# A graph layer's sixty-four-node blocks built in groups of three, with the gather sums in the same ring of PSUM banks

## The reference

```
x: (12500, 128) f32;  src, dst, edge_type: (400000,) int32;  W_data, W_control, W_self: (128, 128)
Xs     = x[src]
m_data = Xs @ W_data.T + b_data
m_ctrl = Xs @ W_control.T + b_control
msg    = where(edge_type == 0, m_data, m_ctrl)
agg    = segment_sum(msg, dst, num_segments=12500)
out    = relu(agg + x @ W_self.T + b_self)
result = layernorm(x + out)          # over the features, no scale or shift
```

## Time and profile before

| | us |
|---|---|
| median of 3 runs | 2782.12 |
| lowest and highest run | 2778.26, 2785.72 |
| the profiled execution, its time | 2784.88 |
| the profiled execution, its span | 2783.0 |
| TensorE busy in the span | 2364.6 |
| VectorE, ScalarE, GpSimd busy | 1266.1, 1224.5, 1691.7 |

### The profile page before, as it was taken

How to read it: one execution, slowest core, us unless ns; L and a number is a source line. 1 busy time by engine, 2 the same in 40 slices (tenths; PEclk the granted TensorE clock), 3 DMA queues, 4 the chain that set the end, 5 groups by cost and what they waited for, 6 DMA issues and landing times.

```text
span 2783.0 us, 47819 instructions
## 1 busy us (share of the span) xinstructions
PE 2364.6 (85%) x17776; PEld 1301.3 (47%) x17776; DVE 1266.1 (45%) x4037; ACT 1224.5 (44%) x1997; POOL 1691.7 (61%) x1785
## 2 busy tenths in 40 slices
PE   3688888888888888888889888988888888888988
PEld 2344444544444444444445454444444444444444
DVE  8444444445444444444444454444444444444443
ACT  6344444444444444444444444444444444444443
POOL 6466665666666665666666666566666666656662
PEclk9899999999999999999999999999999999999999
DMA  7712222222222222222222222222222222222221
GB/s 191 223 47 67 71 72 59 73 68 74 72 73 71 73 72 62 74 69 75 71 72 73 69 75 71 63 69 73 74 69 73 71 73 72 69 61 72 71 75 34
DMA packets 150380, 211.42 MB, mean 76 GB/s; under 512 B 35298, under 2 KB 120725, under 8 KB 150147
## 3 DMA queue, kind: packets, MB, share of 16 engines
q0 software_dynamic: 83232, 170.57, 22.0%
q1 hardware_dynamic: 54177, 28.15, 3.7%
q10 hardware_dynamic: 12738, 9.60, 1.1%
HBM read 189.78 MB, written 18.41 MB: 75 GB/s over the span
## 4 chain that ended last, share of the span: by engine, by line
PE 44%; another core or an unknown queue 23%; ACT 14%; DVE 9%; issue 7%; DVEq 2%; DMA 1%; SPq 0%; ACTq 0%
PE apply_ps L664 25%; ACT cnt L860 13%; PE build L648 8%; PE sum_ps L630 4%; DVEq L1177 2%; DVE hot_q L1136 2%; DVE hot_p L1136 1%; PE misc L673 1%; DVE acc L1183 1%; PE misc L714 1%; DVE sg L1193 1%; PE misc L717 1%; DMA key_dram<-fin 1%; PE misc L692 1%
## 5 line engine op out<-in xcount | busy, mean ns | idle before, releaser
L560 POOL DMA_INDIRECT rows<-x_dram,src_t x1610 | 1524.7, 947 | 947.5 <-issue 383.4
L860 ACT ACTIVATE cnt<-build 128x784 bf16<-128x784 f32 x1408 | 1087.5, 822 | 1457.1 <-remote 773.1
L664 PE MATMUL apply_ps<-x,cnt 128*128 128x385 bf16 x8624 | 1611.2, 337 | 31.0 <-issue 25.5
L664 PEld LDWEIGHTS apply_ps<-x,cnt 128*128 128x128 bf16 x8624 | 868.3, 103 | 604.7 <-issue 135.7
L648 PE MATMUL build<-hot_q,hot_p 64*128 64x196 bf16 x5632 | 425.1, 254 | 274.2 <-ACT cnt L860 205.6
L648 PEld LDWEIGHTS build<-hot_q,hot_p 64*128 64x128 bf16 x5632 | 197.6, 95 | 572.7 <-issue 372.7
L1136 DVE TENSOR_TENSOR hot_q<-const_ps,key_pq 128x784 bf16<-128x784 bf16 x704 | 390.3, 554 | 0.0
L1181 DVE TENSOR_TENSOR acc_deg<-misc,acc_deg 2x32 f32 x346 | 61.9, 179 | 671.2 <-remote 278.7
L1136 DVE TENSOR_TENSOR hot_p<-const_ps,key_pq 128x512 bf16<-128x512 bf16 x704 | 291.2, 414 | 43.1 <-DVE acc L1183 16.5
L560 POOL DMA_INDIRECT rows<-in_x,src_t x120 | 122.8, 1024 | 76.8 <-issue 30.5
L1191 DVE TENSOR_TENSOR zg<-t_mask,sum_ps 128x2 f16<-128x2 f32 x161 | 24.9, 154 | 307.5 <-PE sum_ps L630 158.3
(11 more groups left out here) (182 smaller groups left out, 1082.5 us busy)
## 6 DMA issues: line engine op xcount, KB each, us to landing
rows<-x_dram,src_t POOLq DMA_INDIRECT x1610
x_dram<-x ACTq DMA_DIRECT2D x13, 672.0 KB
cnt<-in_x SPq DMA_DIRECT2D x13, 448.0 KB
x_u<-in_x SPq DMA_DIRECT2D x43, 64.0 KB
out<-out_sb SPq DMA_DIRECT2D x43, 64.0 KB
key_dram<-fin SPq DMA_DIRECT2D x12, 196.5 KB
x_u<-in_x SPq DMA_DIRECT2D x40, 53.5 KB
out<-out_sb SPq DMA_DIRECT2D x40, 53.5 KB
```

The source lines that it names most:

```text
L560: pool.indirect_dma_start(out=rows_f[:, slot, 0:D] if early else rows[:, slot, 0:ROW], out_offset=None, in_=x if early else x3_dram, in_of ...
L664: last = pe.matmul(apply_ps[:, 0:385], cnt[:, k % 2, b, :], x3[:, b, 0:385], start=(b == 0), stop=(b == XBLOCKS - 1))
L860: act.activation(o, i.rearrange("p h (m b) -> p b h m", b=XBLOCKS), ACT.Copy).then_inc(evacuated, 1)
```

## The change

The PSUM tensor of the tables and that of the gather sums go. The tables of line 1136 lie in an SBUF tensor `tables`, and the one of line 1041 in `hot_t`. The four banks become six: `build_ps[0]` to `[2]`, two banks each, used in turn by a list of entries. An entry is a build (now one j) or the sums of a round, in the order in which TensorE makes them; each waits until the entry three before it has been copied out (`evacuated` for a build, `sg_ready` for sums).

Builds come in groups of three, that is twelve nodes. With step s = 3m the group 6m, 6m + 1, 6m + 2 is built at the old place, ahead of the job. With s = 3m + 1 the group 6m + 3 to 6m + 5 is built in the middle of `apply`, which is cut into two halves. With s = 3m + 2 there is none. ScalarE copies the first group out ahead of the step's job and the second behind it.

```
+    def group_at(s):
+        lo = {0: 2 * s, 1: 2 * s + 1}.get(s % 3, 2 * BATCHES)
+        return range(lo, min(lo + 3, 2 * BATCHES))
...
+    entries = []
+    for s in range(STEPS):
+        if s in gather_at:
+            entries.append(("sums", gather_at[s]))
+        entries += [("build", j) for j in group_at(s)]
+    entry = {v: e for e, v in enumerate(entries)}
...
+        hot_t = sb("hot_t", [P, 2 * WIN])
+        tables = sb("tables", [P, P + 2 * XBLOCKS, 2], BF16)
...
-        const_ps = psum("const_ps")
-        build_ps = [psum(f"build{i}", 2 * WIDE) for i in range(2)]
+        build_ps = [psum(f"build{i}", 2 * WIDE) for i in range(BUFFERS)]
         apply_ps = psum("apply_ps")
-        sum_ps = psum("sum_ps")
...
+            def free_banks(who):
+
+                e = entry[who]
+                if e >= BUFFERS:
+                    kind, n = entries[e - BUFFERS]
+                    pe.wait_ge(sg_ready if kind == "sums" else evacuated, n + 1)
+                return build_ps[e % BUFFERS]
...
                 pe.wait_ge(hot_ready, ps + 1)
-                if ps:
-                    pe.wait_ge(sg_ready, ps)
+                if ps == 0:
+                    pe.wait_ge(lists_stored, 2 * len(LISTS))
+                sum_ps = free_banks(("sums", ps))
...
-            def build(n):
-
-                pe.wait_ge(onehot_ready, n + 1)
-                for z in range(2):
-                    j = 2 * n + z
-                    if j >= 2:
-                        pe.wait_ge(evacuated, j - 1)
...
+            def build(j):
+
+                n, z = divmod(j, 2)
                 pe.wait_ge(onehot_ready, n + 1)
+                to = free_banks(("build", j))
+                for i in range(2):
+                    for h in range(2):
+                        half = slice(64 * h, 64 * h + 64)
+                        o = WIDE * h + 2 * XBLOCKS * i
+                        last = pe.matmul(to[:, o:o + 2 * XBLOCKS], hot_p[half, j % 8, :, i],
+                                         hot_q[half, j % 8, :, i], start=True, stop=True)
+                last.then_inc(built, 1)
...
-                b0, b1 = XBLOCKS * c // 8, XBLOCKS * (c + 1) // 8
+                b0, b1 = XBLOCKS * (2 * c + half) // 16, XBLOCKS * (2 * c + half + 1) // 16
...
-                if batch_at(s) is not None:
-                    build(batch_at(s))
+                if s % 3 == 0:
+                    for j in group_at(s):
+                        build(j)
...
-                if 0 <= k < BLOCKS:
-                    apply(k, c)
+                for half in range(2):
+                    if 0 <= k < BLOCKS:
+                        apply(k, c, half)
+                    if half == 0 and s % 3 == 1:
+                        for j in group_at(s):
+                            build(j)
...
-                if batch_at(s) is not None:
-                    evacuate(batch_at(s))
+                if s % 3 == 0:
+                    for j in group_at(s):
+                        evacuate(j)
...
                 if s in turn_at:
                     take_x(turn_at[s])
+                if s % 3 == 1:
+                    for j in group_at(s):
+                        evacuate(j)
...
-            dve.tensor_copy(const_ps[:, HOT], hot_i[:, :])
-            twice_p, twice_q = twice[:, 0:P, :], twice[:, P:P + 2 * XBLOCKS, :]
+            dve.tensor_copy(hot_t[:, :], hot_i[:, :])
             for r in range(2):
-                dve.tensor_copy(twice_p[:, :, r], iota_q[:, 0:P])
-                last = dve.tensor_single_scalar(twice_q[:, :, r], iota_q[:, :], 1.0, ALU.add)
-            step(last)
-            dve.tensor_copy(const_ps[:, TABLES], twice.rearrange("p w r -> p (w r)").bitcast(F32))
+                dve.tensor_copy(table_p[:, :, r], iota_q[:, 0:P])
+                dve.tensor_single_scalar(table_q[:, :, r], iota_q[:, :], 1.0, ALU.add)
```

More of the change, by code:

```diff
@@ L632, in gather_sums, with apply @@
                 last.then_inc(rows_used, 1)
-            def build(n):
+            def build(j):
+                n, z = divmod(j, 2)
                 pe.wait_ge(onehot_ready, n + 1)
-                for z in range(2):
-                    j = 2 * n + z
-                    if j >= 2:
-                        pe.wait_ge(evacuated, j - 1)
[L641 to L652, removed]
-                if c == 0:
+                to = free_banks(("build", j))
[6 more added lines that the diff above has]
+                last.then_inc(built, 1)
+            def apply(k, c, half):
+                if c == 0 and half == 0:
                     pe.wait_ge(evacuated, 16 * (k + 1))
@@ L665, in apply @@
                                      start=(b == 0), stop=(b == XBLOCKS - 1))
-                if c == 7:
+                if c == 7 and half == 1:
                     last.then_inc(applied, 1)
@@ L842, in take_sums @@
                 act.wait_ge(rows_used, ps + 1)
+                sum_ps = build_ps[entry["sums", ps] % BUFFERS]
                 act.activation(sg[:, ps % 2, :], sum_ps[:, 0:D + 1], ACT.Copy).then_inc(act_step, 1)
@@ L846, in take_sums, with evacuate @@
                                scale=sg[:, ps % 2, D:D + 1]).then_inc(sg_ready, 1)
-            def evacuate(n):
-                k = n // 8
-                if n % 8 == 0 and k >= 2:
+            def evacuate(j):
+                k = j // 16
+                if j % 16 == 0 and k >= 2:
                     act.wait_ge(applied, k - 1)
-                if n == 8:
+                if j == 16:
                     act.wait_ge(x3_ready, XCH)
-                for z in range(2):
-                    act.wait_ge(built, 2 * n + z + 1)
-                    c0 = 8 * (2 * (n % 8) + z)
-                    o = cnt[:, k % 2, :, c0:c0 + 8].rearrange("p b (h m) -> p b h m", h=2)
-                    i = build_ps[z][:, :].rearrange("p (h c) -> p h c", h=2)[:, :, 0:4 * XBLOCKS]
-                    act.activation(o, i.rearrange("p h (m b) -> p b h m", b=XBLOCKS), ACT.Copy
-                                   ).then_inc(evacuated, 1)
+                act.wait_ge(built, j + 1)
+                c0 = 8 * (j % 16)
+                o = cnt[:, k % 2, :, c0:c0 + 8].rearrange("p b (h m) -> p b h m", h=2)
+                i = build_ps[entry["build", j] % BUFFERS][:, :].rearrange("p (h c) -> p h c", h=2)[:, :, 0:4 * XBLOCKS]
+                act.activation(o, i.rearrange("p h (m b) -> p b h m", b=XBLOCKS), ACT.Copy).then_inc(evacuated, 1)
             def take_block(k):
```

15 lines of the change are left out of this document (7 added, 8 removed).

## The result

The kernel after takes 2899.95 us (median of 3 runs, 2887.93 to 2904.72) against 2782.12: ratio 1.042, 95% interval [1.036, 1.047], 4% slower where 2% faster was forecast, and outside the range. Its profiled execution took 2887.93 us with a span of 2886.1, at a mean granted clock of 0.94.

What follows compares the result with a forecast made beforehand. No engine is full; TensorE mostly waits for build banks that ScalarE copies late. Terms: -251 us bank waits, -40 insertions, +241 new waits, net -50, so 2782 becomes 2732, rounded 2730 us; range 2600 to 2850.

Steps and rivals of the forecast that it cites:

- Jobs behind three copies: Steps s = 3m, ScalarE copies three builds ahead of the job's bank: 49 waits for `misc`, 29 us more.
- Where s = 3m + 1 the job goes first, which is no worse: Steps s = 3m + 1, ScalarE copies the job out ahead of the group: no added cost.
- a wait also lets the others catch up: Sum of waits: reckoning gave 321 where rows have 251, so excesses of 200 were scaled by 0.78 to 156 us.
- The lag: From the end of a step's first four build matmuls to ScalarE's start: mean 1.23 us, taken as given.
- 62 x 0.78: Plain groups without sums next to them: 297 groups at 0.21 us mean excess, 62 us, scaled by 0.78.
- the third build at s = 0: Third build needs the sums' own banks and waits for VectorE's reduce: 58 x 1.47 = 85 us.
- the sums at s = 8: Sums need the bank of the group's first build, 0.6 us of room: 57 x 0.81 = 46 us.
- at s = 4 the group's third build: Third build against the sums' reduce, 1.95 us of room, 0.26 excess; part of 58 x 0.49 = 28 us.
- Fewer insertions: Changes from `apply` to builds and back fall from 704 to 470, 0.17 us each: 40 us less.
- Tables in SBUF: VectorE's compares get two SBUF inputs and delay GpSimd's gather issues 0.08 us each; no cost, as rounds have room.
- third rival: GpSimd becomes the bound: compares block gather issues, deciding from 0.28 us an issue; about 2850 us, chance 0.07.
- The waits only move: Rival: ScalarE's lateness is kept by jobs and `posted` in place of banks; 2782 us within 10, chance 0.13.
- Sums in the ring cost more: Rival: waits of the third build at s = 0 end in 1.2 GHz spells, 169 to 237 us; about 2850, chance 0.17.

Runs made afterwards that it cites:

- the third job: Job on a chip with held signals, before at 2811.78 us: tables alone 2830.64, with the ring but no groups 2840.71, after 2942.68, after with step breaks 2874.10.
- the ring alone: Kernel after with the grouping undone, two builds in every step, ring and SBUF tables kept: 2840.71 us, 1.010; tables alone were 1.006.
- theory A: Theory tested in the third job: grouping makes chains of gather issues longer, and jobs wait; expected 2750 to 2820 us with grouping undone, measured 2840.71.
- step breaks: Kernel after with GpSimd's quarter waits on a semaphore TensorE raises once a step: 2874.10 us (1.024) with signals held, 2427.34 (1.049) with signals prompt.
- moving the jobs: Kernel after with the job of a step 3m ahead of the three builds, on TensorE and ScalarE: 2911.71 us, 1.039.

## Why the prediction was wrong

**The step that failed** is "Jobs behind three copies", with 29 us and "Where s = 3m + 1 the job goes first, which is no worse". The jobs' waits rose by 184 us, and 176 of the 263 stand in just those steps: 58 ahead of turned node tiles, 47 of blocks, 36 of sums and 35 of outputs. I asked only which copies stand ahead of a job's copy on ScalarE, and took jobs that VectorE frees at nothing. But `misc` comes free only after TensorE's own signal that the job is written, which is held like that of a build, and with builds gone from between two jobs there is one `apply` of 2.15 us to cover it. The idle time was forecast to fall by 10 us and rose by 93. The four lines of jobs alone were off by 161 (184 where 29 x 0.78 = 23 was put), and the builds, sums and `apply` together stayed some 66 under their terms. The same fault is in "a wait also lets the others catch up": 0.78 corrected for it among the builds, while the jobs, behind builds that no longer wait, were left as before.

**The lag** was taken as given, the same with other traffic. The signal's mean delay at the builds did stay about the same (1.06 and 0.93 us). What makes it was open in the prediction and is shown now as far as its trigger: gather issues. It isn't independent from wait to wait, as the sums of excesses had it: in the timeline above one hold strikes TensorE's signals to three engines. In the trace of before only 0.34 of the builds' signals, 0.33 of the jobs' and 0.19 of the sums' come within 0.1 us. ScalarE's own signals are not held: all 377 builds there that stood waiting for a copy began 0.05 to 0.15 us after the end of it.

**The builds.** The bank waits removed were put at 251 of 274 us; the new ones ahead of builds come to 137 (160.0 less the 23 that were to stay), where the terms 62 x 0.78, 85 and 15 of the 28 make 148. By class: the third build at s = 0 waits 67.0 us in 56 of 57 steps (85 forecast), the sums at s = 8 wait 2.3 (46 forecast), and at s = 4 the group's third build 33.9 (58 x 0.26 = 15 forecast). The sum is near because the misses at s = 0 and s = 4 have opposite signs.

**Fewer insertions** was mis-sized. The builds' 46 us less look like the 40 forecast, but most of it comes back as busy time of `apply`. Without gathers, where the clock hardly differs, TensorE as a whole is busy 7 us less, and between the third job's versions with and without groups it is the same within 1 us (2390.3 and 2390.9). **`apply`**: 37.8 us idle, 30 to 60 forecast.

**The clock** was left alone. There are fewer waits but longer ones (533 over 0.1 us became 359, with more idle time), and the spells at 1.2 GHz went from 47 to 76, from 227 us to 348. The prediction's "111 us" are half of the time at that level. An estimate splits the 11 us by which TensorE's busy time rose. It is busy at the lower level for 302 us where it was 188, and 12 `apply` matmuls take 3.60 us there in place of 2.15: 114 x (1 - 2.15 / 3.60) = 46 us more. Each of the 174 waits fewer gives back 0.16 us (a matmul that takes 0.327 us alone adds 0.166 in a run): 28 us less. The insertions are 7 less. So the clock, some 46 us, is the second term missed, and the insertions, 33 short, the third.

Busy time was forecast 40 us lower and came out 11 higher; with the idle time's 103 this makes 154 of the 168 us between forecast and median. The rest is how the profiled runs stand to the medians, 2.8 us above before and 12.0 below after.

**Tables in SBUF.** Issues have a mean of 0.999 us (1.03 forecast), the compares kept theirs, and TensorE never waited for gathers, as forecast. The cost there is 0.6%, not nothing. On a chip with prompt signals the third rival's mechanism holds: 4.1%, at 0.06 us an issue and not 0.28: 2314 us less some 45 around the rounds leave each of 173 13.1 us, so the room over 12.5 is 0.06 an issue.

**The rivals.** "The waits only move" was nearest in mechanism: the ring alone did just that (1.006 to 1.010). "Sums in the ring cost more" was nearest in time, but that was luck, for its place was wrong: 67 us there, not 169 to 237.

**What stays open.** That the groups cost 102 us is shown, why is settled in part. I call a hold the stretch from the fourth issue of a chain to 2.2 us after the start of its last. From 250 us on there are 1054 us of holds with the ring alone and 1027 after, so longer chains aren't it, against my theory A; but TensorE's idle time from 250 us on is 359 us against 447, 1.07 and 1.34 us a wait, and 167 against 227 of it lie inside the holds. Each hold costs more, as I read it because groups leave less work between things that need a signal. With step breaks there are 856 us of holds, which fits what they win back. Where the jobs' waits went fits their distance, but moving the jobs won 0.3 to 0.8 of the 3.6%, and no version here undoes the rest while it keeps the groups. So the distance is argued, not shown, as the cause of the time. After itself wasn't run on a chip with prompt signals. No version with all its gathers beat before on either kind of chip.

## What to carry to other kernels

Before adding buffers against a late signal, ask whether the same lateness strikes the other resources that the waiting engine uses: here it does, and a third buffer for one moved the wait to the one that has a single buffer. Then look at the distance between two uses of that one, for a regrouping may shorten it while it changes nothing else. And if the lateness has a cause outside the engines' work, find it by leaving things out before tuning around it: leaving the gathers out took 17% of this kernel's time, and the change played for 2%.

## What the runs showed of the hardware

**TensorE's signals are held while GpSimd gathers densely, on some chips.** Three of the five chips did so (2777 us; 2812; 2807 and 2784). In the trace of before, the signal of a build with at most one gather issue begun in the 5 us ahead of it came within 0.1 us in all 36 cases, with two in 0.80, with three in 0.45 and with four in 0.08 of 547. With half the gathers it was 0.87, 0.34 and 0.00 with two, three and four; in after's trace of the third job 0.89, 0.46 and 0.10. The delays over 0.5 us end, in the median, 2.2 us after the start of the last issue in the trace of before and 2.1 in after's, but a quarter of after's end within 0.9. On two other chips (2314 us both) 0.96 to 1.00 of the signals came at once even with four issues in 5 us (all of them, if matched in order), and the same kernel is 17% faster. What differs isn't shown by any trace here, nor whether it belongs to the chip or to the time of the job, since only one chip was used twice.

**A part can have very different weights on the two kinds.** The tables cost 0.6% where signals are held and 4.1% where they are prompt. The groups with step breaks cost 1.2% (2874 against 2841 us) and 0.8%; without step breaks, 3.6%, they were timed only where signals are held. A change timed on one kind may say little of the other.
